# First layer's triangle product: blocks of 128 output rows outside, channels inside, with b kept in SBUF as fp16 parts

## What is computed

```python
a = sigmoid((x @ Wa1 + ba1) * (x @ Wa2 + ba2))
b = sigmoid((x @ Wb1 + bb1) * (x @ Wb2 + bb2))
z = einsum('bikc,bkjc->bijc', a, b)
return g * (_ln(z, ln2_g, ln2_b) @ Wz + bz)
```

## Time and profile before

| | us |
|---|---|
| median of three runs | 4713.67 (4711.84 to 4716.98) |
| the profiled execution, its own time | 4714.6 |
| its span in the profile | 4712.9 |
| PE busy in the span | 3987.0 (85%) |
| DVE busy | 3935.2 (83%) |
| ACT busy | 3377.8 (72%) |
| POOL busy | 2670.3 (57%) |

### The profile page before, as it was taken

One profiled execution on the slowest core, in us unless ns is written; L12 is line 12 of the kernel. 1 busy time (PEld: TensorE's weight loads), 2 busy tenths in 40 slices (PEclk: granted clock), 3 DMA queues, 4 the chain that ended last, 5 costly groups with the idle time before them and its releaser, 6 DMA issues. The chain is left out here.

```text
span 4712.9 us, 89415 instructions
## 1 busy us (share of the span) xinstructions
PE 3987.0 (85%) x26438; PEld 2239.9 (48%) x26438; DVE 3935.2 (83%) x5450; ACT 3377.8 (72%) x4840; POOL 2670.3 (57%) x1428
## 2 busy tenths in 40 slices
PE   0008999891999999799999999799999978888888
PEld 0005666441666666455555555355654434444444
DVE  5778888678888888899999999677789978777776
ACT  2337999553777777588888888566667768888887
POOL 0000000591888888588888888733334428888887
PEclk9999999995999999899999999899999989999999
DMA  9997999546999999799999999766678859999999
GB/s 366 410 405 261 364 369 366 176 134 202 392 391 390 390 390 391 268 311 319 321 322 321 320 320 322 271 230 223 231 254 305 305 186 406 407 403 405 403 402 354
DMA packets 700627, 1532.73 MB, mean 325 GB/s; under 512 B 32976, under 2 KB 50832, under 8 KB 698128
## 3 DMA queue, kind: packets, MB, share of 16 engines
q1 hardware_dynamic: 563696, 1263.31, 74.3%
q10 hardware_dynamic: 136864, 268.59, 14.9%
HBM read 1009.59 MB, written 522.19 MB: 325 GB/s over the span
## 5 line engine op out<-in xcount | busy, mean ns | idle before, releaser
L1766 POOL TENSOR_TENSOR s_oT<-s_gated,s7in_x1t 128x1024 f32<-128x1024 f32 x256 | 689.0, 2694 | 220.6 <-DVE s_gated L1685 215.4
L981 POOL TENSOR_TENSOR s_x1T<-s_gz,s_xT 128x512 f32<-128x512 f32 x512 | 652.1, 1274 | 127.9 <-DVE s_gz L947 123.2
L1432 PE MATMUL s_y_ps<-s_ab 128*128 128x512 f16 x3072 | 680.1, 380 | 2.0 <-DVE s_ab L1503 2.0
L1138 POOL TENSOR_TENSOR s_low<-s_xc,s_high 128x1024 f16<-128x1024 f32 x256 | 546.9, 2137 | 222.0 <-ACT s_high L1099 222.0
L878 PE MATMUL s_g_ps<-s_xT,s_Wg 128*128 128x512 f32 x1024 | 523.3, 593 | 0.0
L1685 DVE SCALAR_TENSOR_TENSOR s_gated<-s_p_ps,k_po_bias,s_gate 128x1024 f32<-128x1024 f32 x256 | 328.6, 1284 | 183.7 <-ACT s_gate L1722 164.0
L908 ACT ACTIVATE s_g<-s_g_ps,s_bg 128x512 f32<-128x512 f32 x512 | 351.7, 687 | 174.3 <-PE s_g_ps L878 174.3
L718 POOL MEMSET s_total<- 128x2048 f32 x1 | 1.8, 1809 | 837.9 <-POOLq L41 837.9
L1432 PEld LDWEIGHTS s_y_ps<-s_ab 128*128 128x128 f16 x3072 | 300.9, 98 | 344.8 <-issue 4.4
L947 DVE SCALAR_TENSOR_TENSOR s_gz<-s_z_ps,k_z_bias,s_g 128x512 f32<-128x512 f32 x512 | 384.4, 751 | 88.8 <-ACT s_g L908 86.5
L1104 ACT ACTIVATE s_gate<-s_g_ps,k_gi_bias 128x1024 f32<-128x1024 f32 x256 | 284.1, 1110 | 186.1 <-PE s_g_ps L1272 185.7
(11 more groups left out here) (225 smaller groups left out, 9499.8 us busy)
## 6 DMA issues: line engine op xcount, KB each, us to landing
s2in_xt<-in_x SPq DMA_DIRECT2D x128, 1024.0 KB, 9.6
s_xt<-in_x SPq DMA_DIRECT2D x256, 512.0 KB, 7.3
x_d<-s_x1T ACTq DMA_DIRECT2D x128, 1024.0 KB, 9.6
s5in_xt<-x_d SPq DMA_DIRECT2D x128, 1024.0 KB, 9.1
h_d<-s_h SPq DMA_DIRECT2D x128, 1024.0 KB, 6.8
s7in_x1t<-x_d SPq DMA_DIRECT2D x128, 1024.0 KB, 13.9
out<-s_ot ACTq DMA_DIRECT2D x128, 1024.0 KB, 9.3
s_mask_b<-mask_d SPq DMA_DIRECT2D x128, 512.0 KB, 4.8
```

Source lines behind the costliest of these rows:

```text
L981: pool.tensor_tensor(x1T[:, i // U, i % U, :], gz[:, i % 4, :], xT[:, i % 8, :], ALU.add).then_inc(added, 1)
L1138: pool.tensor_tensor(low[:, n % 4, :, :], xc[:, n % 4, :, :], high[:, n % 4, :, :], ALU.subtract).then_inc(rest_ready, 1)
L1432: last = pe.matmul(y_ps[:, ib, 0:N], ab[:, u % 2, 0, a, kb, ib * P:(ib + 1) * P], ab[:, u % 2, 1, b, kb, :], start=m == 0, stop=m == len(t ...
L1766: pool.tensor_tensor(oT[:, n % 4, :, :], gated[:, n % 4, :, :], x1t[:, n // 2, 2 * (n % 2):2 * (n % 2) + 2, :], ALU.add).then_inc(added, 1)
```

## The change

`stage3_triangle` is written anew; a block of 128 output rows is now outside (`n`), a channel inside (`c`), and one step g = 16 n + c makes one channel of one block:

- `a` is loaded for one block and channel at a time (256 KB, three buffers), turned by four transposes, rounded and split in one piece of 128 x 512. The turn runs two steps ahead of the matmuls.
- `b` of all 16 channels is loaded during block 0 alone, 1 MB in a step behind the step's load of a, into three raw buffers. Two of them lie in `z` (its last eight slots) and one in `spare`. ACT rounds it in one piece of 128 x 2048, DVE makes the rest in one piece. Both parts stay in SBUF in `b` (16 channels x 2 parts) for all four blocks.
- `z` has 24 slots of 128 x 512 in place of 64, so `total`, `total2` and `square` are one piece of 128 x 512 each.
- Blocks 0 to 2 are normalised, rounded, split and stored during the steps of the next block, in eight chunks of two channels. The tables NORM, ROUND and SPLIT give the step of the next block at which each chunk is due. Only block 3 is left for the end. Mean square and deviation are now in PSUM (`mean_ps`, `dev_ps`). The halves of `parts` (in `spare`) wait for the store of the chunk before the last.

The matmuls are the same 768, the transposes the same 256. Each step has its 12 matmuls in a bank of `z_ps`, of which there are three. Beside this, three one-column constants become columns of one tile.

The diff, cut (of the old lines those that a new one answers to; all of them are in the listing above):

```diff
-    AFTER = ((4, 5), (0, 1, 6), (2, 3, 7), ())
+    RB, C, ZS, CHUNK, TERMS = N // P, 16, 24, 2, ((0, 0), (0, 1), (1, 0))
+    CHUNKS, LATER, STEPS = C // CHUNK, C - 1, RB * C
+    NORM, ROUND, SPLIT = (4, 5, 7, 8, 10, 11, 13, 14), (5, 6, 8, 9, 11, 12, 14, 15), (6, 7, 9, 10, 12, 13, 15, 16)
...
+        b = s.sbuf("b", [P, C, 2, RB, N], FP16)
+        spare = s.sbuf("spare", [P, RB * N])
+        z = s.sbuf("z", [P, ZS, N])
+        raw_b = [z[:, C:C + RB, :], z[:, C + RB:C + 2 * RB, :], spare[:].rearrange("p (b j) -> p b j", b=RB)]
...
-                for n in range(2 * C):
-                    sp.dma_start(raw[:, n % SLOTS, :, :], src).then_inc(loaded[n % SLOTS], 16)
+                for g in range(STEPS):
+                    if g >= 3:
+                        sp.wait_ge(turned, g - 2)
+                    sp.dma_start(raw_a[:, g % 3, :], a_v[g // C, g % C]).then_inc(a_loaded[g % 3], 16)
+                    if g < C:
+                        if g >= 3:
+                            sp.wait_ge(b_rest, g - 2)
+                        sp.dma_start(raw_b[g % 3], b_v[C + g]).then_inc(b_loaded[g % 3], 16)
+                    for n, k in due(g - 6, SPLIT):
+                        store(n, k)
...
+                    if g + 2 < STEPS:
+                        turn(g + 2)
+                    pe.wait_ge(a_rest, g + 1)
+                    pe.wait_ge(b_rest, min(g, C - 1) + 1)
+                    before = g - 3
+                    if before >= 0 and before % C == 0:
+                        pe.wait_ge(based, before // C + 1)
+                    elif before >= 0:
+                        pe.wait_ge(taken, later(before))
...
+                def take_square(g):
+                    m = later(g)
+                    act.wait_ge(taken, m)
+                    if m >= 2:
+                        act.wait_ge(summed2, m - 1)
+                    act.activation(square[:], z[:, g % ZS, :], ACT.Square).then_inc(squared, 1)
...
+                def round_z(n, k):
+                    j = CHUNKS * n + k
+                    act.wait_ge(normed, j + 1)
+                    if j >= 2:
+                        act.wait_ge(stored[j % 2], j // 2 * 32)
...
+                for g in range(STEPS):
+                    n, c = g // C, g % C
+                    if g + 1 < C:
+                        rest_b(g + 1)
+                    if g + 2 < STEPS:
+                        rest_a(g + 2)
+                    if c:
+                        take(g)
+                    if n and c == 1:
+                        variance(n - 1)
+                    if n and c == 2:
+                        clear_base(n - 1)
+                    if n and c == 3:
+                        invert(n - 1)
+                    for block_n, k in due(g, SPLIT):
+                        split(block_n, k)
+                    for block_n, k in due(g, NORM):
+                        normalize(block_n, k)
...
-        K.gn_mean, K.gn_scale, K.gn_shift = s.sbuf("gn_mean", [P, 1]), s.sbuf("gn_scale", [P, 1]), s.sbuf("gn_shift", [P, 1])
+        columns = s.sbuf("gn", [P, 4])
+        K.gn_mean, K.gn_scale, K.gn_shift = columns[:, 0:1], columns[:, 1:2], columns[:, 2:3]
```

More of the change, by code:

```diff
@@ L589, in stage3_triangle @@
     b_v = ab_d.rearrange("(p b) c k -> c p b k", b=RB)
-    z_v = z_d.rearrange("(h c) (b p) j -> h b p c j", h=2, p=P)
+    z_v = z_d.rearrange("(h c) (n p) j -> h n p c j", h=2, p=P)
     with ExitStack() as stack:
         s = Scope(nc, stack, "s3")
[L593 to L608, removed]
@@ L610, in _, with later, chunk_of, due @@
+        normed, z_rounded, z_split = s.sem("normed"), s.sem("z_rounded"), s.sem("z_split")
+        def later(g):
+            return LATER * (g // C) + g % C
+        def chunk_of(n, k):
+            first = (C * n + CHUNK * k) % ZS
+            return z[:, first:first + CHUNK, :]
+        def due(step, table):
+            return [(step // C - 1 - e, k) for e in (0, 1) for k, at in enumerate(table)
+                    if at == step % C + C * e and 0 <= step // C - 1 - e < RB - 1]
         @block_of(nc)
@@ L623, in _, with store @@
[L623 to L630, removed]
+                def store(n, k):
+                    j = CHUNKS * n + k
+                    channels = slice(CHUNK * k, CHUNK * k + CHUNK)
+                    for h, ready in ((0, z_rounded), (1, z_split)):
+                        sp.wait_ge(ready, j + 1)
+                        sp.dma_start(z_v[h, n][:, channels, :],
+                                     parts[:, j % 2, h, :, :]).then_inc(stored[j % 2], 16)
@@ L632, in _ @@
+                for step in range(STEPS - 6, STEPS + 1):
+                    for n, k in due(step, SPLIT):
+                        store(n, k)
+                for k in range(CHUNKS):
+                    store(RB - 1, k)
+                for x in range(2):
+                    sp.wait_ge(stored[x], RB * CHUNKS // 2 * 32)
             @block.tensor
             def _(pe):
[L634 to L642, removed]
-                    last.then_inc(turned, 1)
@@ L645, in _, with turn @@
[L645 to L660, removed]
+                def turn(g):
+                    pe.wait_ge(a_loaded[g % 3], g // 3 * 16 + 16)
+                    if g >= 3:
+                        pe.wait_ge(a_rest, g - 2)
+                    for q in range(RB):
+                        last = pe.transpose(t_ps[:, g % 3, q * P:(q + 1) * P], raw_a[:, g % 3, q * P:(q + 1) * P], K.ident[:])
+                    last.then_inc(turned, 1)
@@ new lines, in _ @@
+                for g in range(2):
+                    turn(g)
+                for g in range(STEPS):
[8 more added lines that the diff above has]
+                        pe.wait_ge(taken, later(before))
+                    terms = [(q, x, y) for q in range(RB) for x, y in TERMS]
+                    for m, (q, x, y) in enumerate(terms):
+                        last = pe.matmul(z_ps[:, g % 3, 0:N], a[:, g % 3, x, q * P:(q + 1) * P], b[:, g % C, y, q, :],
+                                         start=m == 0, stop=m == len(terms) - 1)
+                    last.then_inc(product, 1)
@@ L662, in _ @@
             @block.scalar
             def _(act):
[L664 to L675, removed]
@@ L699, in _ @@
[L699 to L711, removed]
@@ L713, in _, with round_a, round_b @@
-                for k in range(2 * RB):
-                    round_z(k)
+                def round_a(g):
+                    act.wait_ge(turned, g + 1)
+                    if g >= 3:
+                        act.wait_ge(product, g - 2)
+                    act.activation(a[:, g % 3, 0, :], t_ps[:, g % 3, 0:N], ACT.Copy).then_inc(a_rounded, 1)
+                def round_b(c):
+                    act.wait_ge(b_loaded[c % 3], c // 3 * 16 + 16)
+                    act.activation(b[:, c, 0, :, :], raw_b[c % 3], ACT.Copy).then_inc(b_rounded, 1)
@@ L792, in stage4_layer0 @@
+                for block_n, k in due(STEPS, SPLIT):
+                    split(block_n, k)
+                last = RB - 1
+                variance(last)
+                clear_base(last)
+                invert(last)
+                normalize(last, 0)
+                for k in range(1, CHUNKS):
+                    normalize(last, k)
+                    split(last, k - 1)
+                split(last, CHUNKS - 1)
 def stage4_layer0(nc, K, x, z_d, x1_d, N, ahead):
```

209 lines of the change are left out of this document (116 added, 93 removed).

## The result

The changed kernel takes 4661.02 us (median of four runs, 4658.82 to 4661.24) against 4712.81 (4711.84 to 4716.98): a ratio of 0.9887, interval 0.987 to 0.9905. That is 51.8 us less; 38 were forecast.

What follows compares the result with a forecast made beforehand. PE was taken to bound the product loop, at 3.03 us a step. Start -3.7, loop +32 and end -66.6 gave -38 against the profiled 4714.6 us: 4677, range 4650 to 4708.

Steps and rivals of the forecast that it cites:

- The end: After the product loop: last sums, scaling to reciprocal, eight chunks, way to stage 4; 33.8 us against 100.4, so -66.6.
- The ring through the stores: End: split 1.1, store 2.3, rounding 0.9, hand-overs and issue 0.5 make 4.8 us for two chunks, over DVE's 4.4.
- Block 0: First 16 steps of the loop: 13 at 5.0 us plus 10 for three without full load, 75 us (54 to 87).
- the floor of 4.66: Block 0: rest of b 2.2 plus POOL's sums 2.46 exclude each other, so no step under 4.66 us.
- The other way to reckon it: Block 0: mean wait of 0.5 added to DVE's 3.4, a step of 3.9 us and block 0 14 us shorter; not used.
- The term of 3.15 a step: Blocks 1 to 3, 48 steps: PE stays the bound by little, 151 us (145 to 168).
- The term put at nothing: SP's list: loads of a stand behind stores of blocks 0 to 2, but six steps ahead of need; cost nothing.
- A: Rival, block 0: the port costs nothing, DVE's 3.4 and PE's 3.03 hold; loop +6, time 4650 us; chance 0.08.
- B: Rival, loop: poor overlap, steps of 5.9 in block 0 and 3.5 behind it; loop +61, time 4705 us; chance 0.13.
- C: Rival, loop: POOL gets both sums in ahead of DVE's port instructions, wait 2.46; loop +91, time 4736 us; chance 0.07.
- D: Rival, block 0: PE's clock falls to the lower level, step 6.3, block 0 101 us, time 4703; chance 0.05.
- E: Rival, block 0: a ahead of b fills the queue, steps at the loads' 6.5 us, time 4697; chance 0.07.

Runs made afterwards that it cites:

- two squares: Changed kernel with a second buffer for ACT's square in block 0, up to the twelfth sum: 4669.1 us, block 0 67.9 us.
- dense chunks: Changed kernel with NORM, ROUND and SPLIT at one chunk a step in place of two in three steps: 4668.5 us, blocks 1 to 3 148.8 us.
- narrow sums: Changed kernel with block 0's sum of values on 8 columns in place of 512 from the third channel on: 4651.9 us, block 0 59.0 us.

## Why the prediction was right

The direction, the mechanism and the place were right; the gain was 14 us larger than forecast (51.8 for 38). Between the two profiled executions it is 53.7, so over 15 more than forecast: 12.4 in the loop and 4.5 outside stage 3, less 1.5 at the start.

- *The end*, forecast at 33.8 and measured at 33.8, agrees by luck: its terms were off by +3.2, -0.7, -0.8 and -1.8, which cancel. The last sums took 5.8 in place of 2.6 (last take 1070.62, scaling 1076.40): three sums were left and not two, and two of them took 2.24 beside the last two splits, with which they excluded each other. The chunks took less than 20.3 (1081.62 to 1101.17: 19.5), the variance 1.8 in place of 2.5, the way from last split to stage 4 3.3 in place of 5.1. The ring through the stores had been put at 4.8 us for two chunks and was 4.55, DVE's own pace: from the end of a split (1085.19) to the rounding that waits for its store (1087.46) it was 2.3, hand-overs and all, where 2.3 and 0.5 had been added up.
- *Block 0* was 68.1 against 75. The step put at 5.0 was 4.50. What failed is "0.3 because `square` has one buffer": the two squares show that this buffer costs nothing, and even the floor of 4.66 was 0.16 too high. The three steps without full load took 11.6 in place of 10; the other thirteen 56.5, 4.35 each, since the first with sums ran at 3.4 while POOL fell behind, and the stall took back most of that. The other way to reckon it, with the mean wait of 0.5, would have given a step of 3.9: the floor was the better guide, 0.16 off against 0.6. Two of the signs came out weaker with it: PE was busy for 78% of block 0 and not for 60 to 65, and the mean rest of b was 2.87, not 3.3, though 3.38 in the steady steps.
- *Blocks 1 to 3* were 145.8 against 151 + 0.7. The term of 3.15 a step was the failing one: no step was longer than PE's 3.03. DVE was busy for 46.2 of 48.5 us in a full block, 45.9 had been added up; the lateness that DVE's cover allows was enough for that, and dense chunks show about where it ends: 4 us late, PE waited 0.75. The term put at nothing, loads of a behind the stores on SP's list, was nothing: between 925 and 1070 us no turn waited for a load.
- *Start*: -2.2 against -3.7 in the first trace; the other eleven runs of the new order that load a first had 11.2 to 12.2, -2.9 to -4.0. So the term holds.
- *Outside stage 3* 4.5 us more were gained (1.35 ahead of it, 3.2 behind), where nothing was changed but the place of three constants. Stage 3 began at 843.8 to 847.3 us in the traces of the new order, and the stretch behind stage 3 took 3552 to 3562 (before: 3558), so nothing shows this to be more than scatter. It is no merit of the forecast.

The rivals: A would have had steps of 3.4 throughout; near that pace came only the narrow sums, which take POOL's work away. B and C: a rest of b took 2.87, not 4.6, and the loop grew by 20, not by 61 or 91. D: the clock did fall once, behind the stall, and was back before the next step's products; over block 0 it was 0.96. E: loads matter only with a buffer less.

## What to carry to other kernels

When work at the end of a stage is moved under its matmuls, add up each engine's list for one period, and beside the lists the resource that two of them share: in block 0 POOL's list (2.46) and DVE's (3.4) would each have allowed steps of 3.4, but what the two may do only by turns came to 4.66 and took 4.50. Cut such work long rather than short if what follows it on the same engine does not need the port: one rest of 2.2 us cost 4.50 a step, four of 0.6 cost 5.75. And a stall that appears once may be an engine catching up: ask whether the busiest one was idle in it before removing it.

## What had not been expected

- Taking turns cost a little less than the sum: a step of rest and two sums took 4.50 where the three add up to 4.66 one after the other. Why isn't shown.
- A sum of 8 columns was recorded with a mean of 1437 ns beside the rests, so an instruction's duration can be nearly all waiting.
- POOL's copy of a square of 128x512 took 0.61 us, its sum of two tiles of that size 1.27.
